# Four cross-attention blocks on one core: the normalising step of the post norms moves to VectorE, and the MLP of a unit runs one phase later

## What is computed

```
def layer_norm(x, g, b, eps):
    m = jnp.mean(x, axis=-1, keepdims=True)
    v = jnp.mean(jnp.square(x - m), axis=-1, keepdims=True)
    return (x - m) * jax.lax.rsqrt(v + eps) * g + b
...
x = mha(q, k, v, self_mask, NUM_HEADS) @ Wo1 + bo1              # layer 3
target = layer_norm(x + target, g1, b1, 1e-05)
x = mha(target @ Wq, context @ Wk, context @ Wv, cross_mask, NUM_HEADS) @ Wo2 + bo2   # layer 4
target = layer_norm(x + target, g2, b2, 1e-05)
h = jax.nn.gelu(target @ W1 + bf1, approximate=False)
x = h @ W2 + bf2
return layer_norm(x + target, g3, b3, 1e-06)
```

## Time and profile before

| what | value |
|---|---|
| median of 3 runs | 2332.77 us (2331.26 to 2337.57) |
| profiled execution | 2326.22 us, span 2323.9 us, mean granted clock 0.981 |
| instructions | 100781 |
| PE busy | 91% of the span |
| DVE busy | 79% |
| ACT busy | 71% |
| POOL busy | 60% |
| DMA | mean 124 GB/s |
| chain that ended last | PE 48%, POOL 20%, SPq 10%, DVE 7%, ACT 6%, issue 5%, DMA 4% |

### The profile page before, as it was taken

How to read it: one execution, slowest core, us unless ns; L and a number is a source line. 1 busy time by engine, 2 the same in 40 slices (tenths; PEclk the granted TensorE clock), 3 DMA queues, 4 the chain that set the end, 5 groups by cost and what they waited for, 6 DMA issues and landing times.

```text
span 2323.9 us, 100781 instructions
## 1 busy us (share of the span) xinstructions
PE 2108.6 (91%) x40685; PEld 1726.2 (74%) x40685; DVE 1829.7 (79%) x4657; ACT 1647.3 (71%) x3278; POOL 1384.1 (60%) x3557
## 2 busy tenths in 40 slices
PE   2789989899999998999999998989999999899987
PEld 2577867687888776777888787768788877677765
DVE  3589887787888887777888888778788889877764
ACT  0367756687887775777888775668788777577775
POOL 3355446886555444888555544688655544488843
PEclk6899999999999999999999999999999999999999
DMA  6355555454555555544555555544455545554432
GB/s 149 91 135 135 134 134 133 113 120 117 131 133 127 136 136 136 125 115 114 133 131 133 129 134 139 131 118 120 117 133 129 123 120 123 136 127 114 120 95 58
DMA packets 310571, 289.18 MB, mean 124 GB/s; under 512 B 50080, under 2 KB 251552, under 8 KB 310112
## 3 DMA queue, kind: packets, MB, share of 16 engines
q1 hardware_dynamic: 305120, 279.80, 48.9%
q10 hardware_dynamic: 4128, 1.65, 0.4%
q0 software_dynamic: 864, 1.28, 0.3%
HBM read 130.51 MB, written 34.60 MB: 71 GB/s over the span
## 4 chain that ended last, share of the span: by engine, by line
PE 48%; POOL 20%; SPq 10%; DVE 7%; ACT 6%; issue 5%; DMA 4%; DVEq 1%; POOLq 0%; ACTq 0%
PE ps_scores_t L837 7%; PE ps_scores L790 6%; PE ps_turn L891 6%; PE ps_turn L821 6%; SPq L531 6%; PE ps_wide L919 5%; PE ps_turn L896 3%; POOL x L645 2%; DVE row_max L1145 2%; PE ps_wide L916 2%; DMA k_slots<-k_dram 2%; PE ps_wide L866 2%; PE ps_wide L867 2%; PE ps_wide L873 2%; POOL post_rstd L603 2%
## 5 line engine op out<-in xcount | busy, mean ns | idle before, releaser
L1145 DVE TENSOR_REDUCE row_max<-ps_scores 128x16 f32<-128x1024 f32 x448 | 547.4, 1222 | 306.3 <-PE ps_scores L790 139.3
L1151 DVE TENSOR_TENSOR shifted<-ps_scores,row_max 128x512 f32<-128x512 f32 x896 | 598.7, 686 | 15.4
L731 ACT ACTIVATE probs<-ps_scores_t 128x512 f32<-128x512 f32 x896 | 486.3, 595 | 79.7 <-PE ps_scores_t L837 77.6
L721 ACT COPY pv_sb<-ps_turn 128x256 f32<-128x256 f32 x448 | 167.0, 373 | 361.5 <-PE ps_turn L821 357.1
L790 PE MATMUL ps_scores<-k_slots,qk_rows 32*64 32x256 f32 x7168 | 311.4, 403 | 49.7 <-DMA k_slots<-k_dram 43.5
L821 PEld LDWEIGHTS ps_turn<-probs,v_ones 128*32 128x32 f32 x14336 | 222.0, 110 | 151.7 <-ACT turned L702 75.9
L837 PE MATMUL ps_scores_t<-ident,shifted 64*128 64x64 f32 x7168 | 321.5, 230 | 11.4 <-DVE attn L1163 7.7
L837 PEld LDWEIGHTS ps_scores_t<-ident,shifted 64*128 64x128 f32 x7168 | 260.0, 140 | 54.9 <-ACT turned L702 9.3
L821 PE MATMUL ps_turn<-probs,v_ones 128*32 128x64 f32 x14336 | 294.7, 223 | 4.2 <-ACT turned L702 2.0
L702 ACT COPY turned<-ps_turn 128x256 f32<-128x256 f32 (+2 forms) x466 | 192.2, 412 | 125.5 <-PE ps_turn L954 111.1
L726 ACT ACT_TABLE_LOAD x190 | 243.8, 1283 | 3.3
(11 more groups left out here) (172 smaller groups left out, 4539.9 us busy)
## 6 DMA issues: line engine op xcount, KB each, us to landing
v_ones<-v_rows SPq DMA_DIRECT2D x1792, 64.0 KB, 2.3
k_slots<-k_dram SPq DMA_DIRECT2D x448, 256.0 KB, 3.3
k_dram<-qk_rows SPq DMA_DIRECT2D x448, 64.0 KB, 2.8
x_in<-in_x SPq DMA_DIRECT2D x64, 64.0 KB, 2.0
ctx_in<-in_ctx SPq DMA_DIRECT2D x64, 64.0 KB, 2.0
out<-x SPq DMA_DIRECT2D x64, 64.0 KB, 1.8
k_dram<-zeros SPq DMA_DIRECT2D x4, 256.0 KB, 6.0
w<-in_L_xattn_W SPq DMA_DIRECT2D x2, 256.0 KB, 6.4
```

The lines of the kernel that those rows point to most:

```text
L731: nc.scalar.activation(probs[:, b, :, :], ps_scores_t[:, b, :] .rearrange("p (h t) -> p h t", t=LEN), ACT.Exp, scale=SCALE).then_inc(probs ...
L1145: v.tensor_reduce(row_max[:, :].rearrange("p (g n) -> p g n", n=SLOTS), ps_scores[:, :, 0:256].rearrange("p g (n k) -> p g n k", k=LEN), A ...
L1151: v.tensor_tensor(shifted[:, j % 2, u, :].rearrange("p (g n k) -> p g n k", n=SLOTS, k=LEN), ps_scores[:, 2 * u:2 * u + 2, 0:256].rearrang ...
```

## The change

`MLP_TURN`, `UP` and `DOWN` become 6, 7 and 8. A post norm's subtract and multiply leave POOL and become one VectorE operation, `post_norm_scale`, a `tensor_scalar` with the mean and the inverse root as its two per-partition operands. It runs one phase after the statistics, behind the second shift, and waits for POOL's power. POOL then has the add of eps and the power in the statistics' phase, and the product with g and the sum with b in the next one, ahead of the roots; these wait for the new semaphores `post_scaled` and `mlp_post_scaled`. The MLP bias moves with them, for all MLP layers. The program has one phase more at its end. MLP norm and pre norm keep their four POOL operations.

```diff
--- before.py
+++ after.py
@@ -56,7 +56,7 @@
 
 QKV, TURN_IN, STATS = 3, 4, 6
 VALUES, TURN_OUT, OUT = 2, 3, 4
-MLP_TURN, UP, DOWN = 5, 6, 7
+MLP_TURN, UP, DOWN = 6, 7, 8
 FIRST = 24
 SCALE = float(HD) ** -0.5
 MASKED = -1e30
@@ -328,9 +328,11 @@
         rows_ready = signal("rows_ready", {n: 2 for n in range(LAYERS) if n != L1_CROSS})
         rope_v_ready = signal("rope_v_ready", {L1_CROSS: 1})
 
-        post_rstd = signal("post_rstd", {n: 5 for n in POST_NORM})
+        post_rstd = signal("post_rstd", {n: 3 for n in POST_NORM})
         mlp_rstd = signal("mlp_rstd", {n: 3 for n in MLP_PRE_NORM})
-        mlp_post_rstd = signal("mlp_post_rstd", {n: 5 for n in MLP_POST_NORM})
+        mlp_post_rstd = signal("mlp_post_rstd", {n: 3 for n in MLP_POST_NORM})
+        post_scaled = signal("post_scaled", {n: 1 for n in POST_NORM})
+        mlp_post_scaled = signal("mlp_post_scaled", {n: 1 for n in MLP_POST_NORM})
         post_x_ready = signal("post_x_ready", {n: 1 for n in POST_NORM})
         mlp_post_x_ready = signal("mlp_post_x_ready", {n: 1 for n in MLP_POST_NORM})
         h_ready = signal("h_ready", {n: 1 for n in PRE_NORM})
@@ -369,7 +371,7 @@
 
             return dram[r, s]
 
-        PHASES = range(-STATS, UNITS + LAG * STREAMS + DOWN + 2)
+        PHASES = range(-STATS, UNITS + LAG * STREAMS + DOWN + 3)
 
         def rounds(phase):
 
@@ -633,16 +635,14 @@
                         normalised(r, j, mlp_norm, x[:, stream_of(j), :]) \
                             .then_inc(mlp_h_ready.sem, MLP_H_STEP)
 
-                def post_norm_end(r, j, norm, g, ready):
-
-                    s, b = stream_of(j), j % RING
-                    inverse_root(r, j, norm)
-                    normalised(r, j, norm, x[:, s, :]).then_inc(norm.root.sem, 1)
-                    pool.wait_ge(norm.root.sem, norm.root.at(r, j, 4))
+                def post_norm_end(r, j, norm, g, scaled, ready):
+
+                    t, b = stream_of(j), j % RING
+                    pool.wait_ge(scaled.sem, scaled.at(r, j))
                     pool.tensor_tensor(norm.normed[:, b, :], norm.normed[:, b, :], post_g[:, g, :],
                                        ALU.mult).then_inc(norm.root.sem, 1)
-                    pool.wait_ge(norm.root.sem, norm.root.at(r, j, 5))
-                    pool.tensor_tensor(x[:, s, :], norm.normed[:, b, :], post_b[:, g, :],
+                    pool.wait_ge(norm.root.sem, norm.root.at(r, j, 3))
+                    pool.tensor_tensor(x[:, t, :], norm.normed[:, b, :], post_b[:, g, :],
                                        ALU.add).then_inc(ready.sem, 1)
 
                 def attention_bias(r, j):
@@ -672,13 +672,20 @@
                     out, down = j - OUT, j - DOWN
                     if exists(r, j + 1):
                         attention_bias(r, j + 1)
+                    if exists(r, down - 1) and layer_of(down - 1) in MLP_POST_NORM:
+                        post_norm_end(r, down - 1, mlp_post_norm, MLP_POST_NORM[layer_of(down - 1)][0],
+                                      mlp_post_scaled, mlp_post_x_ready)
+                    if exists(r, out - 1) and layer_of(out - 1) in POST_NORM:
+                        post_norm_end(r, out - 1, post_norm, POST_NORM[layer_of(out - 1)][0],
+                                      post_scaled, post_x_ready)
+                    if has_mlp(r, out - 1):
+                        mlp_bias(r, out - 1)
                     if exists(r, down) and layer_of(down) in MLP_POST_NORM:
-                        post_norm_end(r, down, mlp_post_norm, MLP_POST_NORM[layer_of(down)][0], mlp_post_x_ready)
+                        inverse_root(r, down, mlp_post_norm)
                     if exists(r, out) and layer_of(out) in POST_NORM:
-                        post_norm_end(r, out, post_norm, POST_NORM[layer_of(out)][0], post_x_ready)
+                        inverse_root(r, out, post_norm)
                     if has_mlp(r, out):
                         mlp_norm_end(r, out)
-                        mlp_bias(r, out)
                     if exists(r, j + STATS):
                         pre_norm_end(r, j + STATS)
 
@@ -1100,6 +1107,13 @@
                                                scalar=norm.mean_var[:, b, 0:1], in1=norm.mean_var[:, b, 1:2],
                                                op0=ALU.mult, op1=ALU.add).then_inc(norm.steps.sem, 1)
 
+                def post_norm_scale(r, j, norm, scaled):
+
+                    b = j % RING
+                    dve.wait_ge(norm.root.sem, norm.root.at(r, j, 2))
+                    v.tensor_scalar(norm.normed[:, b, :], x[:, stream_of(j), :], norm.mean_var[:, b, 0:1],
+                                    norm.rstd[:, b:b + 1], ALU.subtract, ALU.mult).then_inc(scaled.sem, 1)
+
                 def pre_norm_begin(r, j):
                     layer, s = layer_of(j), stream_of(j)
                     if layer not in PRE_NORM:
@@ -1212,6 +1226,11 @@
                         residual(r, j - OUT)
                     if exists(r, j) and not late:
                         shift(r, j, 1)
+                    below, out = j - DOWN - 1, j - OUT - 1
+                    if exists(r, below) and layer_of(below) in MLP_POST_NORM:
+                        post_norm_scale(r, below, mlp_post_norm, mlp_post_scaled)
+                    if exists(r, out) and layer_of(out) in POST_NORM:
+                        post_norm_scale(r, out, post_norm, post_scaled)
                     if has_mlp(r, j - DOWN):
                         mlp_post_norm_begin(r, j - DOWN)
                     if exists(r, j - OUT):
```

## The result

The changed kernel takes 2310.77 us (median; 2309.14 to 2311.34), the one before 2332.02 us in the same comparison (2330.41 to 2337.57): a ratio of 0.9904, interval 0.9886 to 0.9921. The change is worth 21 us, where 12 were forecast: direction and range were right, the size was off by almost a factor of two. The profiled execution of after took 2310.75 us, 15.5 less than the profiled one of before. So the first thing to explain is why two profiles show 15.5 us and the medians 21.

A forecast was written before the change was run, and what follows sets the result against it. TensorE was taken to set the pace, with POOL taking over at long waits. −52 + 31 + 5 + 4 = −12 us against the profiled 2326.2 gave 2314, plus 6.5 to the median: 2321 us, range 2300 to 2346.

The forecast's parts named there:

- What bounds the kernel: TensorE sets the pace over most of the span; POOL takes over where the MLP transpose waits, 42.6 us.
- Parts 1 and 2: Post norm and MLP transpose: POOL loses 46 us of work per round, the transpose gains a phase; together 52 us saved.
- Part 3: VectorE's new scale: 0.25 us each, 0.2 as queue step, no wait added, 0.5 us charged per round.
- my two bounds: Scale's duration: between a supposed two-operand form reading PSUM, 0.426 us, and a tensor_scalar on half the columns, 0.184.
- Part 4: Flipped phase parity: rope meets the up projection 10 times a round, before 3; bill 31 us, plus 5 for context transposes.
- The context rows: Context transposes of layer 0: bad pairs go from 6 to 10 in a round, 0.29 us each, 5 us in all.
- My ±5 for the end: Pipeline's last phases and tail: order changes and a phase without other work is added; nothing counted, within ±5 us.
- Parity nearly free: Rope phases: VectorE's idle time or TensorE running ahead halves the parity bill, giving 2306 us; chance 0.20.
- VectorE held at the scale: Scale meets a running POOL operation or missing power and delays the queue behind it, 24 us more, 2345; chance 0.20.
- Another wait takes the place: Post-norm down phases become VectorE's, the twelve phases stay at 60.3, gain falls by 12, time 2333 us; chance 0.15.
- the last one of the sum: Whole program: adds the 6.5 us between the profiled execution and the median of before, turning 2314 into 2321 us.

The follow-up runs named there:

- the own delay: Changed kernel, but only layer 4's MLP and that of layer 6's first even unit run one phase later, all others at 5, 6, 7: 2278.94 us, ratio 0.9774.
- the products' new place: Changed kernel with the rope products ahead of the second shift in phases without a down projection: 2288.26 us, ratio 0.9813.
- the scale twice: Changed kernel with each VectorE scale done twice, the first result going to a spare tile nobody reads: 2316.03 us, ratio 0.9943.

## Why the prediction was right and where it failed

**What bounds the kernel, Parts 1 and 2: right.** The waits of the earlier trace rows for POOL were the place, and removing them gave 35.6 us in the twelve phases and 18.4 in the four, where 34 and 19 stand in the sum (4 × 8.4 and 4 × 4.7). The twelve phases came out at 56.5 us against 57.3; TensorE's clock stays at 1.00 in them. What the prediction did not see is how the two parts need each other: it let "POOL stops being full" stand beside "the transpose gets a whole phase" as if either would do part of it. Alone they give −6 and +40 us.

**Part 3: the price was too low, the cover was right.** The scale takes 0.34 us, not 0.25:

```profile
L1114 DVE TENSOR_SCALAR post_normed<-x,post_mean_var,post_rstd 128x128 f32<-128x128 f32 x128 | 43.1, 336 | 0.0
...
L1114 DVE TENSOR_SCALAR mlp_post_normed<-x,mlp_post_mean_var,mlp_post_rstd 128x128 f32<-128x128 f32 x64 | 22.8, 357 | 0.0
```

It lay nearer the middle of my two bounds, 0.184 and 0.426. The upper bound was misread: L1021 is no two-operand form, it multiplies by one per-partition operand, and it took 0.43 us for `w_q` but 0.32 to 0.33 for `w` and `w_v` at the same size. Behind a scale the next instruction mostly starts 0.25 to 0.28 us later (0.2 assumed). Counted from where the instruction before has ended, the 192 scales are 50 us of busy time, not 192 × 0.34 = 66. VectorE's sum rises by 36.4 only, since `row_max` now more often starts while the instruction before it is still ending (11 us less counted so) and others overlap a little more. The column of idle time is 0.0: the scale never waited for the power. A second one per norm costs 5 to 9 us in the whole program; I had charged 2 us for the first.

**Part 4: right, a little low.** The rope phases cost 34.0 us against 31, the pairs measured 10.73 as predicted, the up projection waits for the products 40 times as counted (31.3 us, where 24 stood), and the own delay and the products' new place show the cause twice, from both sides. The context rows gave 3.5 instead of 5. My ±5 for the end was too narrow on one side: +5.7, of which 3.9 after the last `row_max`.

**The rivals.** *Parity nearly free*: no, its bill came in full. *VectorE held at the scale*: no, there is no idle time before it, and a second one costs 5 to 9 us (see the scale twice). *Another wait takes the place*, with the twelve phases at 60.3: no, 56.5; that number was reached by the MLP's delay alone (60.1), and there by POOL, not by VectorE.

**The step that failed** is the last one of the sum: "The median of the runs shown, 2332.8, lies 6.5 above the profiled one, so the forecast is 2321". For the profiled execution itself the sum had given 2314, and 2310.75 was measured: 3.5 us off. The other 6.5 us of the 10 come from this step. It carried the difference between one profile and the median over to the new kernel, as if it were time that the change doesn't touch. In the run of before repeated, the profiled execution lay 3.7 us above its median, not below, so the 6.5 us were a low draw of the first profile and no constant. Of the 9.5 us between the two profiles of before, 4.7 lie in the phases that wait for keys and 2.9 in the disturbed twelve. The 2.9 are the lower clock behind the waits for POOL, and these the change removes: after shows 225.8 and 225.9 us in the twelve in its two profiles, at a granted clock of 1.00 in all eight stretches. For the other 6.6 us the cause stays open. After's first profiled run, 2310.75, lies on its median, 2310.77, and its second, 2312.44, on 2312.55; with two draws that may be luck.

**The terms that were mis-sized** against the first profile: the keys' phases −3.6 where I had 0; the twelve −35.6 for −34; against that rope +34 for +31 and the end +5.7 for 0. Against the second profile the keys' phases give −8.3 to −10.0 and the twelve −38.4. Together they take the sum from −12 to between −15.5 and −25. Whether the keys' phases became shorter by the change is not settled: the time before the change scatters by 4.7 us there, the two of after lie 3.6 to 10 below, and no run changed these phases alone. The scores' wait for the keys' DMA did not shrink clearly (43.5 and 46.5 us before, 45.0 and 42.7 after), and the other kernels of this document with the scale on VectorE and a delayed MLP have 361.6 to 365.8 us in this row.

**On contention.** I had a rival by which each scale stands behind a whole POOL operation. In the trace the disturbance is there and small. Four of after's 192 scales, one in each round, take 0.57 to 0.58 us instead of 0.34. One of them:

```profile
1558.96 0.40 POOL L616 TENSOR_TENSOR pre_normed<-pre_normed,pre_rstd 128x128 f32<-128x128 f32 x1
...
1559.29 0.57 DVE L1114 TENSOR_SCALAR mlp_post_normed<-x,mlp_post_mean_var,mlp_post_rstd 128x128 f32<-128x128 f32 x1
...
1559.32 0.46 POOL L661 TENSOR_TENSOR x_bias<-x,b_o_rows 128x128 f32<-128x128 f32 x1
...
1559.94 0.46 POOL L642 TENSOR_TENSOR mlp_post_normed<-mlp_post_normed,post_g 128x128 f32<-128x128 f32 x1 [0.16 <-DVE mlp_post_normed L1114]
```

POOL's L616 is still at work when this scale starts, and L661 starts 0.03 us behind it; both take their usual time. Twenty other scales start 0.18 to 0.19 us into an L661, and four 0.13 us into an L616; these take 0.35 to 0.36 us. The other way round, 48 of the 64 L642 of the MLP post norm start 0.16 us into a scale and take 0.49 us, where all 64 took some 0.456 before. The mean over the 64 scales of the MLP post norm is 0.357 us against 0.336 for the others: 64 × 0.02 = 1.3 us in all. The Trainium skill, "SBUF — State Buffer", section "Who interferes with whom", says that whichever of the two engines issues first holds the shared ports for its whole instruction and the other blocks. That the two disturb each other agrees. A block for the rest of POOL's operation, 0.27 us, does not show in these 24 scales, which are 0.01 to 0.02 us longer than the others; there the measurement decides. The 0.11 us that the prediction set beside this rule belong to L1140, an add of two inputs, and say nothing of a `tensor_scalar`. The rival by that rule, 2345 us, did not occur: POOL waits for the scale in most phases (140 of 192 times) and so is seldom at work beside it, and where it is, little is lost.

## What to carry to other kernels

When stages of a software pipeline are moved by an odd number of phases, list which pairs of stages share a phase and a buffer before and after; the phases' own durations in the old trace can price the new pairs, here to the hundredth (10.73 us). Then ask whether all units need the move: one layer of three did, and moving only that kept the gain and dropped the 34 us. And take the baseline of a sum from more than one execution: here one profile lay 6.5 us below the median, and behind the same waits the clock fell in some rounds and not in others.

## What the runs showed of the hardware

- A `tensor_scalar` of VectorE with two per-partition operands on 128x128 float32 in SBUF takes 0.336 us in the mean of 128 and 0.57 to 0.58 in four, 0.35 to 0.36 in 24 of those that met a running POOL operation; the next VectorE instruction mostly starts 0.25 to 0.28 us after it.
- The program's end can run mostly at TensorE's lower clock in one execution and not in the next: mean granted clock 0.65 or 0.98 behind the last `row_max`, eight matmuls in 2.05 or 1.13 us after the same wait of 0.78 us, and 7 us of the span between them.
- The same waits for POOL (7.3 to 7.4 us in twelve phases) left TensorE's granted clock at 1.00, 0.97 or 0.95 in different rounds of one kernel, and the twelve phases at 64.3, 65.7 or 67.0 us.
- 47 executions of the kernel before spread over 20 us (2318 to 2338), ten of the changed one over 10 (2304.8 to 2315.1); with so unequal numbers this does not show that the changed kernel scatters less. Between two profiles of one kernel the rope, context and quiet stretches repeat within 0.8 us over four rounds; the spread sits in the phases that wait for keys from DMA, in the stretches with long waits for POOL, at the start and at the end.
